# A Swin block and a separable convolution on one core: orders of VectorE and ScalarE around the softmax dealt anew, attention's weighing with the heads mixed

## What is computed

```python
xs = roll(layer_norm(x), (-3, -3)); wins = windows(xs)            # (.., 49, 96)
q, k, v = split(wins @ qkv_w + qkv_b)                             # 3 heads of 32; q *= 32 ** -0.5
attn = softmax(q @ k.T + bias + mask)                             # 49 x 49 per window and head
x = x + roll(unwindows((attn @ v) @ proj_w + proj_b), (3, 3))
x = x + gelu(layer_norm(x) @ fc1_w + fc1_b) @ fc2_w + fc2_b      # hidden 384
y = depthwise3x3(relu(x)) + dw_bias
out = batch_norm(y @ pw_kernel + pw_bias)
```

## Time and profile before

| | us |
|---|---|
| median of 3 runs | 5734.32 (5730.77 to 5737.15) |
| the profiled execution | 5730.71 |
| its span in the trace | 5728.9 |
| PE busy (PEld busy) | 5544.7 (3950.2) |
| DVE busy | 5067.8 |
| ACT busy | 5061.1 |
| POOL busy | 3793.4 |

### The profile page before, as it was taken

The page is one execution under the profiler, slowest core; times in us unless marked ns, Lnnn a source line. Parts: engine busy times, 40 slices in busy tenths (PEclk is TensorE's granted clock), DMA queues, the critical chain, the costliest instruction groups (busy, mean ns, idle before and its releaser), DMA issues.

```text
span 5728.9 us, 202393 instructions
## 1 busy us (share of the span) xinstructions
PE 5544.7 (97%) x81186; PEld 3950.2 (69%) x81186; DVE 5067.8 (88%) x13773; ACT 5061.1 (88%) x11038; POOL 3793.4 (66%) x4105
## 2 busy tenths in 40 slices
PE   5999999999999999999999999999999999999997
PEld 4676767676666676767676776767676767676675
DVE  4989898898989888889898989898888989898987
ACT  4899999998989898999989999999999998999996
POOL 3666666666666666666666666666666666666663
PEclk9999999999999999999999999999999999999998
DMA  1111111111111111111111111111111111111110
GB/s 25 32 34 35 35 34 35 34 35 34 35 34 34 34 35 34 35 34 35 34 34 34 34 34 35 35 34 35 34 35 34 34 34 34 34 34 35 36 35 23
DMA packets 275643, 193.65 MB, mean 34 GB/s; under 512 B 229159, under 2 KB 246040, under 8 KB 274712
## 3 DMA queue, kind: packets, MB, share of 16 engines
q1 hardware_dynamic: 274712, 180.70, 12.0%
HBM read 77.81 MB, written 77.07 MB: 27 GB/s over the span
## 4 chain that ended last, share of the span: by engine, by line
PE 77%; POOL 11%; DVE 9%; issue 2%; SPq 1%; ACT 0%; DVEq 0%; DMA 0%; ACTq 0%; POOLq 0%
PE bank L428 19%; PE bank L446 18%; POOL prob L933 11%; PE bank L483 7%; PE bank L376 6%; PE bank L525 6%; PE bank L394 6%; PE bank L346 5%; DVE vw L836 4%; PE bank L379 3%; PE bank L442 3%; PE bank L464 3%; DVE ssum L803 2%; DVE srec L805 1%; SPq L292 1%
## 5 line engine op out<-in xcount | busy, mean ns | idle before, releaser
L827 DVE SCALAR_TENSOR_TENSOR acc<-ymap,taps,acc 96x784 f32<-96x784 f32 (+2 forms) x2176 | 2140.6, 988 | 54.8
L939 POOL TENSOR_TENSOR rstd<-var_eps,minus_half 112x7 f32<-112x7 f32 x512 | 1113.9, 2176 | 1055.7 <-DVE var_eps L858 1055.7
L428 PE MATMUL bank<-x1T,w 96*128 96x448 f32 (+1 forms) x3072 | 1130.9, 504 | 5.6 <-issue 4.8
L618 ACT ACTIVATE hT<-bank,bfc 128x448 f32<-128x448 f32 (+1 forms) x1536 | 839.2, 577 | 298.6 <-PE bank L428 285.2
L446 PE MATMUL bank<-hT,w 128*96 128x448 f32 (+1 forms) x3072 | 1095.8, 492 | 0.0
L924 POOL TENSOR_TENSOR prob<-prob,smax 128x392 f32<-128x392 f32 x768 | 631.2, 849 | 511.9 <-DVE smax L796 511.9
L949 POOL TENSOR_SCALAR xn<-x_in,minus_mean,rstd 112x96 f32<-112x96 f32 x768 | 865.9, 1137 | 0.0
L933 POOL TENSOR_TENSOR prob<-prob,srec 128x392 f32<-128x392 f32 x768 | 632.8, 852 | 264.1 <-DVE srec L805 264.0
L787 DVE TENSOR_TENSOR prob<-bank,table 128x392 f32<-128x392 f32 x768 | 387.0, 560 | 432.4 <-PE bank L346 432.4
L428 PEld LDWEIGHTS bank<-x1T,w 96*128 96x128 f32 x3072 | 544.4, 190 | 308.3 <-issue 196.2
L446 PEld LDWEIGHTS bank<-hT,w 128*96 128x96 f32 x3072 | 466.6, 163 | 340.9 <-issue 163.4
(11 more groups left out here) (100 smaller groups left out, 10411.7 us busy)
## 6 DMA issues: line engine op xcount, KB each, us to landing
out<-o_tile SPq DMA_DIRECT2D x256, 210.0 KB, 2.5
x_in<-in_x SPq DMA_DIRECT2D x256, 168.0 KB, 2.9
x_in<-in_x SPq DMA_DIRECT2D x256, 126.0 KB, 2.9
k<-qk SPq DMA_DIRECT2D x512, 49.0 KB, 1.9
out<-o_tile SPq DMA_DIRECT2D x256, 84.0 KB, 2.5
hT<-in_L_conv_rel_bias SPq DMA_DIRECT2D x49, 0.6 KB
x1T<-in_L_conv_fc_w SPq DMA_DIRECT2D x1, 144.0 KB, 2.5
w<-in_L_conv_fc_w SPq DMA_DIRECT2D x1, 144.0 KB, 2.3
```

The lines of the kernel that those rows point to most:

```text
L428: pe.matmul(bank[(1, 2, 5)[m]][:, 0:n * PT_], w1[:, m * 128:(m + 1) * 128], x1T[:, first * PT_:(first + n) * PT_], start=True, stop=True). ...
L618: act.activation(hT[:, m, first * PT_:(first + n) * PT_], bank[(1, 2, 5)[m]][:, 0:n * PT_], ACT.Gelu_apprx_tanh, bias=bfc1[:, m:m + 1]).th ...
L827: last = dve.scalar_tensor_tensor(out=dst, in0=src, scalar=taps[:, i:i + 1], in1=dst, op0=ALU.mult, op1=ALU.add)
L939: pool.tensor_tensor(b["rstd"][:], b["var_eps"][:], minus_half[0:PT_], ALU.pow)\
```

## The change

`steps` begins one step earlier (t = -4), since ScalarE's and GpSimd's steps are cut at another place of the cycle: ScalarE's runs from `probs_turned(t, 1)` of one strip to `probs_turned(t + 1, 0)` of the next, GpSimd's from its divisions to the shifts of strip t+1. Within the cycle, GpSimd's order stays the same, but for a wait for its own offset. On ScalarE the keys move behind the second exponential, the output copies behind the third; x1_turned moves behind the three probs_turned; the gelu's table load moves behind attention_out; the first normalisation moves from behind the second table load to between the two halves of the gelus. On VectorE each maximum stands right behind its bias; the sums stand behind the first copy of values and ahead of the second; tap 0 moves behind that second copy; add_x moves from behind tap 6 to behind tap 5; build_table, run once, moves into `values`. On TensorE the weighing first waits for the second copied group, then goes through groups 0 and 1 and, after the third copy, through 2 and 1, so that three neighbouring matmuls belong to three heads. Queries' and keys' matmuls, all shapes and all data stay as they are.

```diff
@@ steps
-    def steps(eng, step, first=-3):
+    def steps(eng, step, first=-4):
...
@@ TensorE
             def turn_probs(t, h):
+                if not has(t):
+                    return
                 wait(pe, p_ready, nth(t, 3, h))
...
-            def weigh_values(t, phase, g):
-                if g == 0:
-                    wait(pe, v_ready, nth(t, 2, 1))
-                    wait(pe, xt_ready, nth(t + 2, 2, 0))
-                    wait(pe, out_ready, nth(t - 4, 2, 1))
-                    if not has(t - 4):
-                        wait(pe, q_ready, nth(t + 1, 2, 1))
-                wait(pe, pt_ready, nth(t, 3, g))
-                for q in range(QUADS):
-                    for side in range(2):
-                        for odd in range(2):
-                            rows = slice(64 * odd, 64 * odd + NT)
-                            at = (2 * q + side) * NT
-                            h = HEAD_OF[g][q // 2]
-                            mm = pe.matmul(bank[(4, 0)[odd]][h * HD:(h + 1) * HD, at:at + NT],
-                                           vw[rows, phase % 2, q, side, h * HD:(h + 1) * HD],
-                                           probT[rows, g, q, 64 * side:64 * side + NT], start=True, stop=True)
-                if g == HEADS - 1:
-                    mm.then_inc(o_psum, 1)
+            def weigh_one(phase, g, q, side, odd):
+                rows = slice(64 * odd, 64 * odd + NT)
+                at = (2 * q + side) * NT
+                h = HEAD_OF[g][q // 2]
+                return pe.matmul(bank[(4, 0)[odd]][h * HD:(h + 1) * HD, at:at + NT],
+                                 vw[rows, phase % 2, q, side, h * HD:(h + 1) * HD],
+                                 probT[rows, g, q, 64 * side:64 * side + NT], start=True, stop=True)
+            def weigh_values(t, phase):
+                if not has(t):
+                    return
+                wait(pe, v_ready, nth(t, 2, 1))
+                wait(pe, xt_ready, nth(t + 2, 2, 0))
+                wait(pe, out_ready, nth(t - 4, 2, 1))
+                if not has(t - 4):
+                    wait(pe, q_ready, nth(t + 1, 2, 1))
+                wait(pe, pt_ready, nth(t, 3, 1))
+                tiles = [(q, side, odd) for q in range(2) for side in range(2) for odd in range(2)]
+                for q, side, odd in tiles:
+                    weigh_one(phase, 0, q, side, odd)
+                    weigh_one(phase, 0, q + 2, side, odd)
+                    weigh_one(phase, 1, q, side, odd)
+                wait(pe, pt_ready, nth(t, 3, 2))
+                for q, side, odd in tiles:
+                    weigh_one(phase, 2, q, side, odd)
+                    weigh_one(phase, 2, q + 2, side, odd)
+                    mm = weigh_one(phase, 1, q + 2, side, odd)
+                mm.then_inc(o_psum, 1)
...
                 pointwise(t, phase, 1)
                 turn_x(t)
                 turn_x1(t)
-                if has(t):
-                    for h in range(HEADS):
-                        turn_probs(t, h)
-                    for h in range(HEADS):
-                        weigh_values(t, phase, h)
+                turn_probs(t, 0)
+                turn_probs(t, 1)
+                turn_probs(t, 2)
+                weigh_values(t, phase)
                 hidden(t, 0)
...
@@ ScalarE
-            def gelus(t):
+            def gelus(t, half):
                 if not has(t - 1):
                     return
-                wait(act, y_psum, nth(t - 2, 2, 1))
-                for i in range(2 * MC):
-                    half, m = i // MC, i % MC
+                wait(act, y_psum, nth(t - 2, 2, half))
+                for i in range(MC * half, MC * (half + 1)):
+                    m = i % MC
...
-            def step(t, phase):
-                queries(t)
-                keys(t)
-                exps(t, 0)
-                exps(t, 1)
-                outputs(t, phase, 0)
-                exps(t, 2)
-                outputs(t, phase, 1)
-                x_turned(t, 0)
-                x_turned(t, 1)
-                x1_turned(t)
-                for h in range(HEADS):
-                    probs_turned(t, h)
+            def load_gelu(t):
                 if has(t - 1):
                     act.activation(table_load[:, 1:2], table_load[:, 0:1], ACT.Gelu_apprx_tanh)
-                attention_out(t)
-                gelus(t)
+            def load_exp(t):
                 if has(t + 1):
                     act.activation(table_load[:, 1:2], table_load[:, 0:1], ACT.Exp)
+            def first_norm(t, phase):
                 if has(t + 3):
                     wait(act, xt_psum, nth(t + 2, 2, 1))
                     normalise(0, t + 3, xn, x_in[:, (phase + 3) % UNROLL], xn_ready)
-                into_map(t, 0)
-                into_map(t, 1)
+            def second_norm(t):
                 if has(t):
                     wait(act, x1t_psum, nth(t - 1, 2, 1))
                     normalise(1, t, x1n, x1[:, t % 2], x1n_ready)
+            def step(t, phase):
+                probs_turned(t, 1)
+                probs_turned(t, 2)
+                x1_turned(t)
+                attention_out(t)
+                load_gelu(t)
+                gelus(t, 0)
+                first_norm(t, phase)
+                gelus(t, 1)
+                load_exp(t)
+                into_map(t, 0)
+                into_map(t, 1)
+                second_norm(t)
+                queries(t + 1)
+                exps(t + 1, 0)
+                exps(t + 1, 1)
+                keys(t + 1)
+                exps(t + 1, 2)
+                outputs(t + 1, (phase + 1) % UNROLL, 0)
+                outputs(t + 1, (phase + 1) % UNROLL, 1)
+                x_turned(t + 1, 0)
+                x_turned(t + 1, 1)
+                probs_turned(t + 1, 0)
...
@@ VectorE
             def values(t, phase, i):
+                if t == -1 and i == 1:
+                    build_table()
...
             def step(t, phase):
-                for g in range(3):
-                    add_bias(t, phase, g)
-                for g in range(3):
-                    find_max(t, g)
+                add_bias(t, phase, 0)
+                find_max(t, 0)
+                add_bias(t, phase, 1)
+                find_max(t, 1)
+                add_bias(t, phase, 2)
+                find_max(t, 2)
+                values(t, phase, 0)
+                add_up(t, 0)
+                add_up(t, 1)
+                add_up(t, 2)
+                values(t, phase, 1)
                 tap(t, phase, 0)
-                values(t, phase, 0)
-                values(t, phase, 1)
-                if t == -1:
-                    build_table()
-                for g in range(3):
-                    add_up(t, g)
                 norm_x(t, phase)
-                for i in range(1, 7):
-                    tap(t, phase, i)
+                tap(t, phase, 1)
+                tap(t, phase, 2)
+                tap(t, phase, 3)
+                tap(t, phase, 4)
+                tap(t, phase, 5)
                 add_x(t, phase)
+                tap(t, phase, 6)
                 tap(t, phase, 7)
                 tap(t, phase, 8)
...
@@ GpSimd
-            def rest(which, dst, src, done):
+            def rest(which, s, dst, src, done):
                 b = ln[which]
+                wait(pool, scale_ready[which], nth(s, 1, 0))
                 for j in range(ACT_NORM, WS):
                     last = pool.tensor_scalar(dst[:, j], src[:, j], b["minus_mean"][:, j:j + 1],
                                               b["rstd"][:, j:j + 1], ALU.add, ALU.mult)
                 last.then_inc(done, 1)
-            def step(t, phase):
-                for g in range(3):
-                    shift(t, g)
-                for g in range(3):
-                    divide(t, g)
+            def first_scale(t):
                 if has(t + 3):
                     root(0, t + 3)
-                    wait(pool, xt_psum, nth(t + 2, 2, 1))
-                    rest(0, xn, x_in[:, (phase + 3) % UNROLL], xn_rest)
+            def second_scale(t):
                 if has(t):
                     root(1, t)
+            def first_rest(t, phase):
+                if has(t + 3):
+                    wait(pool, xt_psum, nth(t + 2, 2, 1))
+                    rest(0, t + 3, xn, x_in[:, (phase + 3) % UNROLL], xn_rest)
+            def second_rest(t):
+                if has(t):
                     wait(pool, x1t_psum, nth(t - 1, 2, 1))
-                    rest(1, x1n, x1[:, t % 2], x1n_rest)
+                    rest(1, t, x1n, x1[:, t % 2], x1n_rest)
+            def step(t, phase):
+                divide(t, 0)
+                divide(t, 1)
+                divide(t, 2)
+                first_scale(t)
+                first_rest(t, phase)
+                second_scale(t)
+                second_rest(t)
+                shift(t + 1, 0)
+                shift(t + 1, 1)
+                shift(t + 1, 2)
             steps(pool, step)
```

## The result

The changed kernel takes 5499.2 us (median of 4 runs, 5488.5 to 5513.9) against 5735.3 us: the ratio is 0.959, with a 95% interval of 0.957 to 0.962. The forecast was 5513 us, 0.3% above. The profiled execution took 5488.5 us, its span is 5486.8.

The account below looks back on a forecast made before the run. TensorE, busy 97%, was taken as the bound: S+9.58 plus 11.46 us gives 21.04 us a strip instead of 21.89, 218 us less over 256 strips. From 5730.7 that is 5513 us, own range 5460 to 5560.

Parts of the forecast that it names:

- TensorE's idle time of 0.8 us goes: TensorE's detour per strip, waiting for GpSimd's divisions before transposing probabilities, vanishes: 0.8 us, with 0.3 to 0.9 in hand.
- S: The end of a strip's scores on TensorE; S+6.6 means 6.6 us later.
- New wait before the weighing, start at S+8.23: TensorE's weighing begins when the second copy of turned probabilities is there, 0.3 us after TensorE could.
- First hidden matmul at S+9.58: On TensorE it waits for ScalarE's x1 copy, ending at S+9.50; today it starts at S+10.43.
- 11.46 us from there to the next S: From the first hidden matmul to the next end of scores, all TensorE's; forecast to stay 11.46 us.
- the second sign that I had named for being wrong: The first hidden matmul's way to the next S no longer 11.46 us, meaning a gelu or the map comes late.
- The sum: Strip time: 9.58 + 11.46 = 21.04 us in place of 21.89, 0.85 less; 218 us over 256 strips.
- What the mixing brings: Heads mixed in TensorE's weighing, 1.66 to 1.25 us: 0.31 of the 0.85 us, 0.1 hidden by the x1 copy.
- Shifts beside biases: GpSimd's shifts running beside VectorE's biases: at most 0.4 us of waiting each, taken as nothing.
- rival 3: VectorE or ScalarE becomes the bound, with two GpSimd chains (shifts, second offset) beside new instructions: 5616 us, chance 0.12.
- VectorE's reserve: VectorE's slack, its wait for scores: from 1.67 us a strip down to some 0.4.
- Rivals 1, 2 and 4: Mixed weighing stays 16.6 ns/pass (5592 us, chance 0.13); is slower (5884 us, 0.06); divisions end no earlier (5725 us, 0.03).

## Why the prediction was right, step by step

- **TensorE's idle time of 0.8 us goes.** Right. The divisions were forecast to end at S+7.1 and end at 7.12; maxima stand 1.07 apart; the idle time for them fell from 338 to 19.5 us. It was worth more than 0.8: in the run without the mixing the old weighing starts at S+7.76 (median) against 8.77, since twelve transposes without a pause also take less than the 1.56 us that I gave them. The runs with the sums late and with VectorE's order alone show that this needs the sums' place and that it isn't enough.
- **New wait before the weighing, start at S+8.23.** It is S+8.17, with 0.35 us of waiting for the turned copy against 0.3 forecast.
- **First hidden matmul at S+9.58.** It is S+9.29, so this is the step whose sizes failed: I had written that I am wrong if it comes before S+9.4. The order of events was right, two terms were too long. A pass of the weighing was taken at the scores' 12.3 ns and takes 10.2, outside the 11 to 13 that I gave; but the x1 copy comes last, so this alone moves nothing. The term that counts is the time of the copies. The third turned copy was put at S+8.69; it ends at 3018.44 = S+8.46, because twelve transposes without a pause take 1.46 us, (1.46 - 0.26) / 11 = 0.11 from start to start, where I had read 0.13 off groups of four, and the copies follow each other accordingly. The x1 copies then end at 3019.22 = S+9.24, and the hidden matmul follows 0.05 later.
- **11.46 us from there to the next S.** It is 3030.84 - 3019.27 = 11.57, the second sign that I had named for being wrong, and a gelu is late as it said. The first gelu was to be there 0.3 us before it was needed, and it is in time: it ends at 3022.28 + 0.61 = 3022.89, and its loads start at 3023.00. The second gelu, which I had not looked at, ends at about 3023.41, and the loads that need it start at 3023.46, after 0.16 us of waiting for it; that half takes 1.81 in place of 1.72. The table load behind the attention outputs was in ScalarE's sum, but its cost to TensorE was put at nothing; ScalarE's order alone costs 0.20 us there, and in the changed kernel 0.1.
- **The sum.** 9.29 + 11.57 = 20.86 against 21.04. 256 x (21.89 - 20.86) is 264 us; the spans differ by 242, the medians by 236. What is missing are single strips that are longer, told of below: what strips take beyond the median strip adds up to 12 us before and 36 after. The gain was forecast at 218 us and came out at 236; by the regular strip it would have been 264. That the time fits better than the strip is luck.
- **What the mixing brings.** I had 0.31 us a strip (79 us); taking it out costs 40 us. The failed step is that I left the new wait for the second copy in the sum without the mixing. The old weighing needs only the first copy and starts at S+7.76 in place of 8.23, with the first hidden matmul at S+9.42 in place of 9.89 (medians). By strips the mixing brings 0.23 us: 0.12 of them up to the hidden matmul, the rest behind it.
- **Shifts beside biases.** Taken at nothing. GpSimd's mean for a shift is 851 ns against 849 before, so rival 3's first half is out. Its other half was near: GpSimd's second offset ends at 3009.07 + 0.78 = 3009.85, and ScalarE's normalisation that reads it starts at 3009.94.
- **VectorE's reserve.** Forecast 0.4 us a strip; its wait for the scores is 70.0 us in 190 strips, 0.37:

```profile
L810 DVE TENSOR_TENSOR prob<-bank,table 128x392 f32<-128x392 f32 x570 | 319.6, 561 | 70.1 <-PE bank L346 70.0
```

- **Rivals 1, 2 and 4.** The mixing works (1 and 2 out, by the weight loads), and the orders do what they say (4 out).

## What to carry to other kernels

Where one engine is nearly full and waits at one place, write down the times at which it asks for each input and the times at which each arrives: what an order is worth is the move of the latest one, so orders on two engines can be worth 0.7% and -0.9% each by itself and 3.4% together. When a step is moved behind another on a helper engine, count also who waits for what stands behind it (here the table load, the gelus, and a matmul two stages later). Small matmuls should go around several tiles of the array: here one, two, three and six tiles at work gave 37, 16.6, 12.6 and 10.2 ns a pass, so most of the gain is there with three.

## What the chip showed that I had not expected

Six tiles take a pass every 10 ns, closer than anything in the kernel before, though the scores use six tiles too and take 12.3; the scores' weights have 49 columns where these have 32. That this is the reason was not tried.

A few strips are long. In the changed kernel one takes 28.0 us. TensorE pauses there 2.32 us behind the weighing, for nothing that the profile shows, and then its granted clock is half for about 10 us. Timeline of TensorE, and then the windows (length, busy us of each engine with counts, granted clock, DMA):

```profile
4463.97 1.09 PE L474 MATMUL bank<-probT,vw 49*32 49x49 f32 x96 [0.36 <-ACT probT L635]
4467.38 3.21 PE L428 MATMUL bank<-x1T,w 96*128 96x448 f32 x6 [2.32 <-issue]
```

```profile
4464.00:4466.00 2.00, 1.05 (x96) 1.10 (x97) 1.90 (x11) 1.88 (x6) 0.81 (x1) 1.00 0.04 8
4466.00:4468.00 2.00, 0.62 (x2) 0.38 (x2) 1.93 (x4) 1.97 (x7) 1.74 (x3) 1.00 0.00 0
4468.00:4470.00 2.00, 2.00 (x5) 1.02 (x4) 1.93 (x5) 1.42 (x3) 2.00 (x3) 0.71 0.00 0
4470.00:4472.00 2.00, 2.00 (x10) 1.62 (x9) 0.99 (x2) 1.38 (x4) 1.12 (x1) 0.50 0.00 0
...
4478.00:4480.00 2.00, 2.00 (x6) 0.77 (x5) 1.27 (x3) 0.67 (x2) 1.82 (x4) 0.73 0.00 0
4480.00:4482.00 2.00, 2.00 (x10) 1.22 (x9) 0.00 (x0) 1.31 (x2) 0.25 (x1) 1.00 0.00 0
```

The clock goes from 2.4 to 1.2 GHz (granted 0.50) behind a stretch in which TensorE was busy for 0.62 of 2 us, and returns while it is fully busy. The strip costs 28.0 - 20.9 = 7 us. The kernel before has the same at 1860 us, with a pause of 1.56 us, in a strip of 25.1 us. The mean granted clock is 0.997 in the profiled run of before, 0.990 to 0.996 in its 17 later runs, and 0.987 to 0.993 in the four runs of the changed kernel; the slowest of those (5513.9 us) has 0.987 and the fastest (5488.5) 0.993, though the two between stand the other way round. Pauses of over 1 us at this place between 100 and 5400 us: three in the trace of before (up to 1.56 us), four in that of the changed kernel (up to 2.32), with the clock at half behind one and two of them. Why the pause comes, and whether the changed kernel draws more of them, stays open: these are single traces, and no run here was made for it.
